# Local layers: first feed-forward matrix in two rounded parts, row norms by logarithm and exponential

## The chip, the cores and the metric

The kernel runs on one core of a Trainium2 chip. The metric is the device time of one execution in microseconds (us). Engines in the rows are named PE (TensorE), PEld (its weight loads), DVE (VectorE), ACT (ScalarE), POOL (GpSimd) and SP (SyncE, which issues DMAs).

## The reference, cut to what matters

Four blocks follow each other, each with a residual and a layer norm: an attention with relative positions, a stack of six local layers, a causal attention, and a mixture of experts. The change lies almost wholly in the six local layers, which for 16 sequences of 256 rows and 128 columns compute:

```python
def attn_layer(x, Wqkv, qs, ksc, Wo):      # 16 heads of 64
    q, k, v = heads(x @ Wqkv)
    q = l2norm(q) * qs                     # t / max(norm(t), 1e-12)
    k = l2norm(k) * ksc
    q = q * cos * scale + rotate_half(q) * sin * scale
    k = k * cos * inv + rotate_half(k) * sin * inv
    return local_attention(q, k, v) @ Wo   # window of 32, scale 8.0

def ffn_layer(x, g, bln, W1, b1, W2, b2):  # W1 is 128 x 682, W2 341 x 128
    xn = (x - mu) / jnp.sqrt(var + 1e-05) * g + bln
    a, gate = jnp.split(xn @ W1 + b1, 2, -1)
    return a * jax.nn.gelu(gate, approximate=False) @ W2 + b2

for i in range(6):
    x = attn_layer(shift_tokens(x), ...) + x
    x = ffn_layer(shift_tokens(x), ...) + x
```

## The kernel before

All activations of the 16 sequences stay on the chip, in `X`. The local layers run sequence by sequence and layer by layer: a *pass* `one_pass(l, b)` belongs to layer `l` and sequence `b` (`n = l * 16 + b`), and 96 of them follow each other. Each pass has four *slots*, j = 0 to 3. A step is one half of the heads for one half of the rows (128 rows, 8 heads of queries and 8 of keys), so a sequence has four steps. In slot j the engines work on different steps at once: the projections of step j + 4, turned queries and keys and scores of step j + 2, probabilities and outputs of step j + 1, and the product with Wo of step j. The feed forward of the sequence before (`f = n - 1`) is spread over the slots. Passes 2 to 13 of each layer are a hardware loop; the others are written out.

There is no scheduler. Each engine has its own program, written out in order, and semaphores join them. The order on each engine in a slot:

- TensorE (`one_pass`): projections of queries and keys (`by_high` L1544 and L1545, `by_low` L1549), turning of the scaled rows (`turn_qk` L1533), projection of values, in slot 2 `first_gates`, in slot 3 `first_values`, then `turn_outputs` (L1579, waits for the query copy two steps on), `turn_probs` (L1593), `scores` (L1612), in slot 2 `last_gate_and_value`, `through_wo` (L1631), `outputs` (L1641), and at the end of slot 1 `turn_xn` (L1652). `through_w1` (L1658) multiplies two chunks of the first matrix, in float32, with the turned normalised rows `xnT`; it is called three times a pass. `ffn_output` (L1681) stands in slot 0 of the pass after.
- ScalarE: `exps` (L1821), `mask` (L1825), `squares` (L1798), the copies of turned queries and keys (L1785, L1787), values (L1807), in slot 2 two `gated` (L1843), turned outputs and probabilities (L1816, L1812); at the end of slot 1 `scale_x` (L1832) and `turned_xn` (L1837), in slot 2 the third `gated`, in slot 3 `turned_x` (L1780). In slot 2 a tiny GELU (L1793) ahead of the squares loads the GELU's table; the first exponential after it loads its own again.
- VectorE: `rotate` (L1943 to L1945, sums of squares L1950), maxima and their subtraction (L1962, L1966, into `b_pr`), `floor_squares` (L1956), `normalise`, `residual`, and the feed forward's statistics and gates.
- GpSimd: for each step `normalise_rows`: the sum of the rotation's two products (L1416), the inverse norms by a power of -0.5 (L1420), in the first step of a pass the feed forward's `deviations` (L1433 to L1438, whose last result `shift` ScalarE needs for `scale_x`), and the scaling of the rows (L1427). After the second step `split_x` (L1444, L1447) makes the rounded high and low part of a later sequence's input. In the last two passes of a layer it also makes the low parts of the next layer's projection weights (`low_part`, L1410, 128 x 512 each) and the tables with gains.
- SyncE: loads, window copies of values, and the shifted copy `x_shifted` (`shift_x`). `load_w1` for a layer is issued in the layer's second pass, once the values of the layer before are through.

For the input and the projection weights the kernel already uses two rounded parts (type `F32R`, "fp32r" in the rows): x·w is computed as high·high + high·low + low·high. TensorE waits at each step's first use of the new layer's weights for `w_low`, which counts the low parts, six a layer.

Of the kernel before, what the change touches and what calls it, by code (L numbers as in the profile page):

```python
# [57 lines left out]
def shape_constants():  # L58
# [39 lines left out]
    c["rot_cos"] = lay(cos * scale * f(8), cos * inv)  # L98
    c["rot_sin"] = lay(sin * scale * f(8), sin * inv)
# [32 lines left out]
def build_program(nc, T, out):  # L132
    ctx = ExitStack()
    with ctx:
# [106 lines left out]
        with ExitStack() as st:  # L241
# [42 lines left out]
            ev_wr, tabs = sem("a_ev_wr"), sem("a_tabs")  # L284
# [6 lines left out]
            ROW, EXT, PRODUCT, PP, CHAIN = 2, 3, 4, 5, 6  # L291
            E_HIGH, E_LOW, EK_MASKED, EK_HIGH, EK_LOW = 6, 7, 8, 9, 11

            x_copied, queries_ok = sem("a_x_copied"), sem("a_queries_ok")
            far = sem("a_far")
# [6 lines left out]
            with nc.Block() as block:  # L302
                @block.sync
                def _(sp):
# [6 lines left out]
                    for name, t in (("L0_attn_Ek", 1), ("L0_attn_Eq", 2)):  # L311
# [12 lines left out]
                    sp.dma_start(tab_ext.rearrange("t d r -> d t r"), ext[:, 0:2, :]).then_inc(tabs, 16)  # L324
                    sp.wait_ge(tabs, 16)
                    sp.dma_start(ek_row, bass.AP(tab_ext, HD * NREX + KREV,
                                                 [[0, P // HD], [NREX, HD], [1, KJ]])).then_inc(tabs, 16)
                    sp.dma_start(eq_tab[:, :], bass.AP(tab_ext, 0, [[1, LB], [NREX, HD], [1, TABW]])).then_inc(tabs, 16)
                    sp.wait_ge(tabs, 16 * 3)
# [3 lines left out]
                def _(act):  # L333
# [6 lines left out]
                    for t in range(LT):  # L340
                        act.dma_start(e_col[:, t:t + 1], bass.AP(T["L0_attn_Eq"].tensor, t * (NREL - 1) * HD,
                                                                 [[0, P // HD], [1, HD], [1, 1]]),
                                      allow_slow_non_contiguous=True).then_inc(far, 16)
                        row = (1 - t) * (NREL - 1)
                        act.dma_start(ev_far[:, t, :], T["L0_attn_Ev"][row:row + 1, :].broadcast_to((P, HD))
                                      ).then_inc(far, 16)
# [8 lines left out]
                def _(pool):  # L355
# [11 lines left out]
                    pool.wait_ge(far, 16 * 2 * LT)  # L367
# [7 lines left out]
                    pool.wait_ge(ld_w, 48)  # L375
# [7 lines left out]
                    pool.wait_ge(tabs, 16 * 3)  # L383
# [773 lines left out]
        with ExitStack() as st:  # L1157
# [9 lines left out]
            w1 = sb(st, "b_w1", [P, 2 * FF])  # L1167
            w2 = sb(st, "b_w2", [P, 3, D])
# [8 lines left out]
            rnorm = sb(st, "b_rnorm", [P, 2, 16])  # L1177
            t1, t2 = sb(st, "b_t1", [P, 2, 16, BD]), sb(st, "b_t2", [P, 2, 16, BD])
# [45 lines left out]
            masked = sem("b_masked")  # L1224

            N_WA, N_LN, N_W1, N_W2 = 3, 2, 5, 3
            SEQ = 4
# [29 lines left out]
            with nc.Block() as block:  # L1257
# [148 lines left out]
                def _(pool):  # L1406
# [6 lines left out]
                    def normalise_rows(n, s, deviations_of=None):  # L1413
# [46 lines left out]
                    def one_pass(l, b, front=True, ffn=True, last_front=False, new_front=False, x_follows=True,  # L1460
                                 last_norm=False):
# [1396 lines left out]
```

## Time and profile before

| | us |
|---|---|
| median of 3 runs | 5004.2 |
| lowest, highest | 5002.4, 5008.55 |
| the profiled execution's own time | 5004.04 |
| its span, from first to last instruction | 5002.2 |
| PE busy | 4560.0 |
| PEld busy | 3754.4 |
| VectorE busy | 3696.6 |
| ScalarE busy | 3399.6 |
| GpSimd busy | 3558.5 |

Busy time is what the engine's instructions cover in the span; matmuls are pipelined and their ends are modelled, so for them the distance between starts tells more than a duration. The time outside the span is 1.8 us. The mean granted TensorE clock was 0.972 of full speed. The local layers take the span from about 960 to 4230 us, ahead of them is the first attention, behind them the causal attention and the experts.

### The profile page before, as it was taken

How to read it: one execution, taken by the hardware profiler on the slowest of the kernel's cores; microseconds unless marked ns; L12 is line 12 of the kernel's file. 1: busy time of each engine (PE TensorE's matmuls, PEld its weight loads, DVE VectorE, ACT ScalarE, POOL GpSimd, SP SyncE). 2: the span in 40 equal slices, each digit the busy share in tenths (PEclk: the TensorE clock that was granted, in tenths of full speed). 3: DMA queues.
4: the chain of work that ended last, by engine and by line, in shares of the span. 5: the costliest groups of instructions: out<-in, count | busy, mean ns of one | idle time of the engine just before them, and what ended most of it. 6: DMA issues, size and time to landing. Idle time of an engine off the chain costs nothing. (4 is left out here: it accounts for less than half of the span.)

```text
span 5002.2 us, 202509 instructions
## 1 busy us (share of the span) xinstructions
PE 4560.0 (91%) x82160; PEld 3754.4 (75%) x82160; DVE 3696.6 (74%) x7406; ACT 3399.6 (68%) x6468; POOL 3558.5 (71%) x2507
## 2 busy tenths in 40 slices
PE   6888888799999999999999999999999997888879
PEld 4777777678887888788877887888877885555557
DVE  4877777788887888778877888788877884555544
ACT  3565565577777777777777777777777774666664
POOL 3334334499999999989999999999999995222212
PEclk8999999999999999999999999999999998999889
DMA  4333333332223222332223222322232221000000
GB/s 119 98 101 112 98 104 105 93 84 69 68 69 88 70 68 69 73 83 69 69 72 85 70 69 70 87 69 70 68 74 70 69 68 40 1 0 0 0 1 18
DMA packets 500471, 338.98 MB, mean 68 GB/s; under 512 B 222559, under 2 KB 489084, under 8 KB 499213
## 3 DMA queue, kind: packets, MB, share of 16 engines
q1 hardware_dynamic: 493566, 320.55, 25.3%
q10 hardware_dynamic: 6544, 13.18, 0.9%
q8 instruction: 280, 4.59, 0.4%
q14 instruction: 81, 0.66, 0.0%
HBM read 60.06 MB, written 54.58 MB: 23 GB/s over the span
## 5 line engine op out<-in xcount | busy, mean ns | idle before, releaser
L1420 POOL TENSOR_TENSOR b_rnorm<-b_ss,neghalf 128x16 f32<-128x16 f32 x384 | 1118.2, 2912 | 25.1 <-DVE b_ss L1956 21.5
L1416 POOL TENSOR_TENSOR b_rot<-b_t 128x1024 f32<-128x1024 f32 x384 | 909.5, 2369 | 75.3 <-DVE b_t L1945 74.6
L1943 DVE TENSOR_TENSOR b_t<-psum,b_cosg 128x1024 f32<-128x1024 f32 x384 | 469.6, 1223 | 426.3 <-ACT b_sq L1798 420.3
L1427 POOL TENSOR_TENSOR b_qk<-b_rot,b_rnorm 128x1024 f32<-128x1024 f32 x384 | 731.0, 1904 | 42.8 <-POOL b_rnorm L1420 2.7
L1544 PE MATMUL psum<-b_w_hi,b_xT_parts 128*128 128x512 f32 x1152 | 528.0, 458 | 28.6 <-issue 19.3
L1798 ACT ACTIVATE b_sq<-psum 128x1024 f32<-128x1024 f32 x384 | 392.1, 1021 | 221.9 <-PE psum L1549 221.5
L1950 DVE TENSOR_REDUCE b_ss_floor<-b_sq 128x16 f32<-128x1024 f32 x384 | 464.3, 1209 | 0.0
L1549 PE MATMUL psum<-b_w_hi,b_xT_parts 128*128 128x512 f32 x1152 | 459.9, 399 | 0.0
L1545 PE MATMUL psum<-b_w_lo,b_xT_parts 128*128 128x512 f32 x1152 | 457.3, 397 | 0.0
L1631 PE MATMUL psum<-shared,b_oT 128*128 128x128 f32 x3072 | 425.2, 281 | 0.8 <-ACT b_oT L1816 0.8
L1533 PE MATMUL psum<-ident,b_qk 128*128 128x128 f32 x3072 | 405.9, 275 | 21.3 <-DVE b_o L1982 15.3
L1533 PEld LDWEIGHTS psum<-ident,b_qk 128*128 128x128 f32 x3072 | 360.0, 142 | 84.9 <-DVE b_o L1982 25.7
L1631 PEld LDWEIGHTS psum<-shared,b_oT 128*128 128x128 f32 x3072 | 380.0, 191 | 27.2 <-issue 1.5
L1821 ACT ACTIVATE b_pr<-b_pr 128x512 f32<-128x512 f32 x384 | 241.6, 629 | 217.0 <-DVE b_pr L1966 197.2
L1982 DVE TENSOR_TENSOR b_o<-psum,b_rs 128x256 f32<-128x256 f32 x768 | 326.2, 425 | 26.5
L1641 PE MATMUL psum<-b_v_win,b_prT 64*32 64x65 f32 x24576 | 336.4, 225 | 3.9 <-issue 3.8
L1612 PE MATMUL psum<-b_kT,b_qTs 64*32 64x64 f32 x24576 | 333.3, 224 | 0.4 <-issue 0.4
L1658 PE MATMUL psum<-b_xnT,b_w 128*128 128x256 f32 (+1 forms) x1152 | 306.2, 388 | 16.8 <-DVE b_hid L2006 2.9
L1612 PEld LDWEIGHTS psum<-b_kT,b_qTs 64*32 64x32 f32 x24576 | 270.6, 105 | 61.5 <-issue 49.4
L1641 PEld LDWEIGHTS psum<-b_v_win,b_prT 64*32 64x32 f32 x24576 | 272.1, 105 | 51.5 <-issue 5.0
L1816 ACT COPY b_oT<-psum 128x512 f32<-128x512 f32 x384 | 232.5, 605 | 112.6 <-PE psum L1579 112.5
L2357 ACT ACTIVATE c_probs<-psum,c_nmax 128x256 f32<-128x256 f32 x512 | 200.9, 482 | 117.5 <-DVE c_nmax L2424 117.2
(271 smaller groups left out, 11545.8 us busy)
## 6 DMA issues: line engine op xcount, KB each, us to landing
b_v_win<-b_v SPq DMA_DIRECT2D x2304, 65.0 KB
keyed<-shared SPq DMA_DIRECT2D x64, 768.0 KB, 4.7
b_v_win<-b_v SPq DMA_DIRECT2D x1152, 32.5 KB
a_logits<-keyed SPq DMA_DIRECT2D x128, 160.0 KB, 3.1
oa<-XR SPq DMA_DIRECT2D x1024, 2.0 KB
xcur<-X SPq DMA_DIRECT2D x111, 128.0 KB, 4.3
shared<-in_L_ffn_Wqkv_dram ACTq DMA_DIRECT2D x6, 1536.0 KB
a_logits<-keyed SPq DMA_DIRECT2D x64, 128.0 KB, 3.0
```

The costliest lines, as they stand in the source:

```text
L1416: nc.gpsimd.tensor_tensor(rot[:, i, :, :], t1[:, i, :, :], t2[:, i, :, :], ALU.add).then_inc(rot_done, 1)
L1420: nc.gpsimd.tensor_tensor(rnorm[:, i, :], ss[:, i, :], neghalf[:, :], ALU.pow).then_inc(rn_done, 1)
L1427: nc.gpsimd.tensor_tensor(qk[:, i, :, :], rot[:, i, :, :], rnorm[:, i, :, None].broadcast_to((P, 16, BD)), ALU.mult).then_inc(qk_done, 1)
L1533: last = nc.tensor.transpose(r[:, p * P:(p + 1) * P], qk[:, s % 2, a * 8 + 2 * p:a * 8 + 2 * p + 2, :].rearrange("p h d -> p (h d)"), iden ...
L1544: nc.tensor.matmul(r, xT_hi[:, ts], w_hi[:, piece(hg, i)], start=True, stop=False)
L1545: nc.tensor.matmul(r, xT_hi[:, ts], w_lo[:, piece(hg, i)], start=False, stop=False)
L1549: return nc.tensor.matmul(r, xT_lo[:, ts], w_hi[:, piece(hg, i)], start=False, stop=True)
L1612: last = nc.tensor.matmul(bank[3 + j][qs, p * 2 * WIN:(p + 1) * 2 * WIN], qTs[at, p, qs], kT[at, p, keys], start=False, stop=(p == 3), ski ...
L1631: last = nc.tensor.matmul(bank_c[:, 0:D], oT[:, p, :], wo[:, 4 * (s % SEQ // 2) + p, :], start=(p == 0), stop=(p == 3))
L1641: last = nc.tensor.matmul(r[qs, p * (BD + 1):(p + 1) * (BD + 1)], prT[at, p, qs], v_win[at, s % NV, c, p, :], start=(p == 0), stop=(p == 3 ...
L1943: nc.vector.tensor_tensor(t14, x4, tab(cosg, slice(0, BD), BD), ALU.mult)
L1950: nc.vector.tensor_reduce(ss_floor[:, t, :, 0], sq[:, :].rearrange("p (h d) -> p h d", d=BD), AX.X, ALU.add).then_inc(ss_done, 1)
```

## The change

The feed forward's first product is computed like the projections. Once a layer GpSimd splits `w1` into `w1_hi` and `w1_lo` (`split_w1`), behind `split_x` in the second step of the layer's second pass. ScalarE reads the turned normalised rows twice, once into `xnT` in float32 and once rounded into `xn_parts[:, 0]`, and GpSimd makes the low part (`split_xn`) in the second step of every pass, between the rotation's sum and the norms. `through_w1` issues three rounded matmuls for each chunk instead of one in float32, and `first_gates` waits for the low part and, in a layer's first feed forward, for the split of `w1`. The counter `w_low` now counts eight a layer.

The inverse norms of the rows are computed as exp(-0.5 · ln(s)) on ScalarE (`guess_norms`), followed by one step of Newton's method on GpSimd, r·(3 - s·r²), which gives twice the inverse norm; the tables of the rotation take the factor 0.5. The set of activation tables that holds both functions is loaded by name at the start and in slot 3 of each pass with a feed forward. In the first attention, two semaphores are dropped and their loads counted on others (L284 to L383).

```diff
-    c["rot_cos"] = lay(cos * scale * f(8), cos * inv)
-    c["rot_sin"] = lay(sin * scale * f(8), sin * inv)
+    c["rot_cos"] = lay(cos * scale * f(4), cos * inv * f(0.5))
+    c["rot_sin"] = lay(sin * scale * f(4), sin * inv * f(0.5))
...
-                    pool.wait_ge(far, 16 * 2 * LT)
+                    pool.wait_ge(ld_w, 16 * (3 + 2 * LT))
...
-                    def normalise_rows(n, s, deviations_of=None):
+                    def normalise_rows(n, s, deviations_of=None, split_of=None):
                         m, i = n * SEQ + s + 1, s % 2
                         pool.wait_ge(t_done, m)
                         nc.gpsimd.tensor_tensor(rot[:, i, :, :], t1[:, i, :, :], t2[:, i, :, :],
                                                 ALU.add).then_inc(rot_done, 1)
-
-                        pool.wait_ge(floor_done, m)
-                        nc.gpsimd.tensor_tensor(rnorm[:, i, :], ss[:, i, :], neghalf[:, :],
-                                                ALU.pow).then_inc(rn_done, 1)
+                        if split_of is not None:
+                            split_xn(split_of)
+                        pool.wait_ge(guess_done, 2 * m)
+                        nc.gpsimd.tensor_tensor(rn_step[:, i, :], ss[:, i, :], rn_guess[:, i, :], ALU.mult).then_inc(step_done, 1)
+                        pool.wait_ge(step_done, 3 * m - 2)
+                        nc.gpsimd.tensor_tensor(rn_step[:, i, :], rn_step[:, i, :], rn_guess[:, i, :], ALU.mult).then_inc(step_done, 1)
+                        pool.wait_ge(step_done, 3 * m - 1)
+                        nc.gpsimd.tensor_tensor(rn_step[:, i, :], three[:, :], rn_step[:, i, :], ALU.subtract).then_inc(step_done, 1)
+                        pool.wait_ge(step_done, 3 * m)
+                        nc.gpsimd.tensor_tensor(rnorm[:, i, :], rn_step[:, i, :], rn_guess[:, i, :], ALU.mult).then_inc(rn_done, 1)
...
+                    def split_xn(f):
+                        pool.wait_ge(xnT_done, 2 * f + 2)
+                        nc.gpsimd.tensor_tensor(xn_parts[:, 1, :], xnT[:, :], xn_parts[:, 0, :].bitcast(F32),
+                                                ALU.subtract).then_inc(xn_split, 1)
+
+                    def split_w1(l):
+
+                        both = slice(0, 2 * FF)
+                        pool.wait_ge(w1_ld, (l + 1) * (16 * N_W1))
+                        nc.gpsimd.tensor_tensor(w1_hi[:, both], w1[:, :], ones[:, 0:1].broadcast_to((P, 2 * FF)),
+                                                ALU.mult).then_inc(w_low, 1)
+                        pool.wait_ge(w_low, l * N_LOW + 7)
+                        nc.gpsimd.tensor_tensor(w1_lo[:, both], w1[:, :], w1_hi[:, both].bitcast(F32),
+                                                ALU.subtract).then_inc(w_low, 1)
...
                             if front:
-                                normalise_rows(n + 1, s, n - 1 if ffn and s == 0 else None)
+                                normalise_rows(n + 1, s, n - 1 if ffn and s == 0 else None,
+                                               n - 1 if ffn and s == 1 else None)
                             if last_front and s == 0:
                                 layer_gains(l + 1)
                             if x_follows and s == 1:
                                 split_x(n + 2)
+                            if new_ffn and s == 1:
+                                split_w1(l)
...
                             w, k = FCH[c % 3], (c // 3) * FF + P * (c % 3)
-                            last = nc.tensor.matmul(ffn_bank[0:w, j * S:(j + 1) * S], w1[:, k:k + w], xnT[:, :],
-                                                    start=(j == 0), stop=(j == 1), skip_group_check=True)
+                            w += w % 2
+                            for i, (weight, part) in enumerate(((w1_hi, 0), (w1_lo, 0), (w1_hi, 1))):
+                                last = nc.tensor.matmul(ffn_bank[0:w, j * S:(j + 1) * S], weight[:, k:k + w],
+                                                        xn_parts[:, part, :], start=(j == 0 and i == 0),
+                                                        stop=(j == 1 and i == 2), skip_group_check=True)
                         last.then_inc(h_full, 1)
 
                     def first_gates(f, new_ffn):
                         if new_ffn is not None:
-                            pe.wait_ge(w1_ld, (new_ffn + 1) * (16 * N_W1))
-                        pe.wait_ge(xnT_done, f + 1)
+                            pe.wait_ge(w_low, (new_ffn + 1) * N_LOW)
+                        pe.wait_ge(xn_split, f + 1)
                         through_w1(3, 4)
...
+                    def guess_norms(s, m):
+
+                        i = s % 2
+                        act.wait_ge(floor_done, m)
+                        nc.scalar.activation(log_ss[:, i, :], ss[:, i, :], ACT.Ln).then_inc(guess_done, 1)
+                        act.wait_ge(guess_done, 2 * m - 1)
+                        nc.scalar.activation(rn_guess[:, i, :], log_ss[:, i, :], ACT.Exp, scale=-0.5).then_inc(guess_done, 1)
+
...
                         nc.scalar.activation(xnT[:, :], ffn_bank[:, 0:S], ACT.Identity, bias=lnb[:, 0:1],
                                              scale=lng[:, 0:1]).then_inc(xnT_done, 1)
+                        nc.scalar.activation(xn_parts[:, 0, :], ffn_bank[:, 0:S], ACT.Identity, bias=lnb[:, 0:1],
+                                             scale=lng[:, 0:1]).then_inc(xnT_done, 1)
...
+                            if j == 3 and ffn:
+                                nc.scalar.preload_act_table_set(LOG_EXP)
                             if ok(j + 1):
                                 exps(j + 1, m + 1)
+                            if ok(j + 3):
+                                guess_norms(j + 3, m + 3)
```

## Rows read from the trace of the kernel before

**Rows 1.** Busy time in a stretch: us, each engine busy (x count), clock, DMA share, GB/s

```profile
2000.00:2500.00 500.00, 482.79 (x10019) 403.29 (x10017) 400.76 (x860) 371.19 (x645) 467.70 (x278) 0.99 0.30 73
```

**Rows 2.** TensorE's waits, 1000 to 4230: in total, times, longest us

```profile
PE psum L1579 <- ACT b_qTs L1785: 20.1, 86, 0.3
...
PE psum L1533 <- POOL b_qk L1427: 3.8, 4, 1.7
```

**Rows 3.** Timeline of TensorE, one pass: start us, us, line, out<-in, count, idle before

```profile
2418.81 0.44 PE L1652 MATMUL psum<-ident,b_xn 128*128 128x128 f32 x2
...
2422.05 1.03 PE L1658 MATMUL psum<-b_xnT,b_w 128*128 128x256 f32 x4
2423.33 0.66 PE L1579 MATMUL psum<-ident,b_o 128*128 128x128 f32 x4 [0.25 <-ACT b_qTs L1785]
...
2425.57 1.09 PE L1658 MATMUL psum<-b_xnT,b_w 128*85 128x256 f32 x4
...
2431.34 1.02 PE L1658 MATMUL psum<-b_xnT,b_w 128*128 128x256 f32 x4
2432.20 0.60 PE L1579 MATMUL psum<-ident,b_o 128*128 128x128 f32 x4
```

**Rows 4.** Timeline of ScalarE, the same pass

```profile
2419.29 0.57 ACT L1837 ACTIVATE b_xnT<-psum,b_lnb,b_lng 128x256 f32<-128x256 f32 x1 [1.56 <-PE psum L1652]
2419.75 0.62 ACT L1821 ACTIVATE b_pr<-b_pr 128x512 f32<-128x512 f32 x1
...
2422.70 0.58 ACT L1785 COPY b_qTs<-psum 128x512 f32<-128x512 f32 x1
...
2424.64 0.87 ACT L1843 ACTIVATE b_gel<-psum,b_b 128x256 f32<-128x256 f32 x2
...
2429.97 1.02 ACT L1798 ACTIVATE b_sq<-psum 128x1024 f32<-128x1024 f32 x1 [0.37 <-PE psum L1549]
```

**Rows 5.** Timeline of TensorE in phase one

```profile
604.56 0.27 PE L654 MATMUL psum<-a_k_diag,a_e_parts 128*128 128x256 f32 x1
...
604.91 0.40 PE L650 MATMUL psum<-a_k_diag,a_q_parts 128*128 128x256 f32 x2
```

**Rows 6.** One line, L650: duration ns least, median, most

```profile
L650 PEld LDWEIGHTS psum<-a_k_diag,a_q_parts x512: 186/189/337, 67.3 to 947.2; 128*128 128x128 f32 x171
```

**Rows 7.** Groups of instructions, 1000 to 4230: count, busy us, mean ns

```profile
L1793 ACT ACT_TABLE_LOAD x94 | 120.6, 1283 | 1.7
...
L1410 POOL TENSOR_TENSOR b_w_lo<-shared,b_w_hi 128x512 fp32r<-128x512 f32 x30 | 38.2, 1287 | 0.0
...
L1793 ACT ACTIVATE b_no_gate<-ones 128x1 f32<-128x1 f32 x94 | 19.2, 204 | 1.1
```

**Rows 8.** The page's costliest groups: count, busy us, mean ns, idle before

```profile
L1420 POOL TENSOR_TENSOR b_rnorm<-b_ss,neghalf 128x16 f32<-128x16 f32 x384 | 1118.2, 2912 | 25.1 <-DVE b_ss L1956 21.5
...
L1427 POOL TENSOR_TENSOR b_qk<-b_rot,b_rnorm 128x1024 f32<-128x1024 f32 x384 | 731.0, 1904 | 42.8 <-POOL b_rnorm L1420 2.7
```

**Rows 9.** Timeline of GpSimd, the same pass as rows 3

```profile
2414.90 0.69 POOL L1436 TENSOR_TENSOR b_frstd<-b_fvar,neghalf 128x2 f32<-128x2 f32 x1
2415.68 0.20 POOL L1438 TENSOR_TENSOR b_shift<-b_less_mean,b_frstd 128x2 f32<-128x2 f32 x1
```

**Rows 10.** Timeline of TensorE, last pass of the first layer

```profile
1514.53 0.41 PE L1652 MATMUL psum<-ident,b_xn 128*128 128x128 f32 x2 [4.24 <-ACT b_xn L1832]
```

**Rows 11.** Timeline of ScalarE, last pass of the first layer

```profile
1513.51 0.88 ACT L1832 ACTIVATE b_xn<-b_x_shifted,b_shift,b_frstd 128x128 f32<-128x128 f32 x2 [5.13 <-POOL b_shift L1438]
```

**Rows 12.** Busy time behind that gap; the last but two numbers are clock, DMA share

```profile
1514.00:1518.00 4.00, 3.47 (x13) 2.87 (x14) 0.00 (x0) 3.38 (x6) 4.00 (x3) 0.63 0.38 89
```

**Rows 13.** Timeline of GpSimd, second pass of the second layer

```profile
1581.11 2.39 POOL L1416 TENSOR_TENSOR b_rot<-b_t 128x1024 f32<-128x1024 f32 x1
...
1588.37 0.61 POOL L1444 TENSOR_TENSOR b_x_parts<-xcur,ones 128x256 fp32r<-128x256 f32 x1
```

**Rows 14.** Timeline of TensorE, second pass of the second layer

```profile
1585.14 1.03 PE L1658 MATMUL psum<-b_xnT,b_w 128*128 128x256 f32 x4
```

More of the change, by code:

```diff
@@ L291, in build_program @@
             ROW, EXT, PRODUCT, PP, CHAIN = 2, 3, 4, 5, 6
+            TURNED, TABLES = 4, 6
             E_HIGH, E_LOW, EK_MASKED, EK_HIGH, EK_LOW = 6, 7, 8, 9, 11
             x_copied, queries_ok = sem("a_x_copied"), sem("a_queries_ok")
-            far = sem("a_far")
             def window_blocks(mt, hh):
@@ L342, in _ @@
                                                                  [[0, P // HD], [1, HD], [1, 1]]),
-                                      allow_slow_non_contiguous=True).then_inc(far, 16)
+                                      allow_slow_non_contiguous=True).then_inc(ld_w, 16)
                         row = (1 - t) * (NREL - 1)
                         act.dma_start(ev_far[:, t, :], T["L0_attn_Ev"][row:row + 1, :].broadcast_to((P, HD))
-                                      ).then_inc(far, 16)
+                                      ).then_inc(ld_w, 16)
                     act.dma_start(X[:, :, :], x_in).then_inc(ld_x, 16)
@@ L1167, in build_program @@
             w1 = sb(st, "b_w1", [P, 2 * FF])
+            w1_hi, w1_lo = sb(st, "b_w1_hi", [P, 2 * FF + 2], F32R), sb(st, "b_w1_lo", [P, 2 * FF + 2], F32R)
+            xn_parts = sb(st, "b_xn_parts", [P, 2, S], F32R)
             w2 = sb(st, "b_w2", [P, 3, D])
@@ L1177, in build_program @@
             rnorm = sb(st, "b_rnorm", [P, 2, 16])
+            log_ss, rn_guess, rn_step = (sb(st, f"b_{n}", [P, 2, 16]) for n in ("log_ss", "rn_guess", "rn_step"))
+            three = sb(st, "b_three", [P, 16])
             t1, t2 = sb(st, "b_t1", [P, 2, 16, BD]), sb(st, "b_t2", [P, 2, 16, BD])
@@ L1223, in build_program @@
             gel_done, hid_done = sem("b_gel_done"), sem("b_hid_done")
-            masked = sem("b_masked")
+            masked, xn_split = sem("b_masked"), sem("b_xn_split")
+            guess_done, step_done = sem("b_guess_done"), sem("b_step_done")
+            LOG_EXP = "natural_log_exp_and_others"
             N_WA, N_LN, N_W1, N_W2 = 3, 2, 5, 3
+            N_LOW = 6 + 2
             SEQ = 4
@@ L1469, in one_pass @@
                                 split_x(n + 2)
+                            if new_ffn and s == 1:
+                                split_w1(l)
                             if ffn and s == 0 and not front:
                                 deviations(n - 1)
+                            if ffn and s == 1 and not front:
+                                split_xn(n - 1)
                             if last_front and s == 1:
@@ L1486, in _ @@
                     nc.gpsimd.memset(zero[:, :], 0.0)
+                    for parts in (w1_hi, w1_lo):
+                        nc.gpsimd.tensor_tensor(parts[:, 2 * FF:], ones[:, 0:2], ones[:, 0:2], ALU.subtract)
+                    nc.gpsimd.memset(three[:, :], 3.0)
                     nc.gpsimd.memset(ss_floor[:, :, :, 1], 1e-24).then_inc(filled, 1)
```

27 lines of the change are left out of this document (14 added, 13 removed).

## The prediction, as it was put on record

> **What bounds the kernel now.** I began with the busy times of a stretch inside the local layers, where nearly all of the change lies: of 500 us TensorE works 482.8 and GpSimd 467.7 [rows 1]. The reader is to see that both look like a bound. The table of waits decides: in the whole stage TensorE waited for GpSimd's scaled rows 4 times, 3.8 us in all, but for ScalarE's copy of the queries, at L1579, 86 times in 96 passes [rows 2]. GpSimd works 94% of the time, yet ahead of need.
>
> A pass (one sequence, four slots) takes about 33 us. Its chain, from the timelines: TensorE turns the normalised rows at 2418.81 (L1652). Projections, turned rows and the first gates follow, the gates from 2422.05; L1579 starts at 2423.33, just as the queries' copy ends, 2422.70 + 0.58 [rows 3, 4]. From 2419.29 on ScalarE has no gap: turned rows, exponentials, a table load, squares, queries. So in slot 2 the chain runs through ScalarE; a second place is the pair of gates at 2425.57, right behind the GELU's end, 2424.64 + 0.87 [rows 3, 4]. From there to the next L1652 it is TensorE's own work.
>
> **The change, part by part.** *TensorE.* A pair of chunks is 4 instructions now; the pair at 2431.34 lets L1579 begin at 2432.20: 0.86 us [rows 3]. After it is 6 rounded matmuls of 256 columns. Phase one has such matmuls, same size of weights and columns: three steps from 604.56 to 604.91, 0.117 us each [rows 5]. 6 x 0.117 = 0.70, a gain of 0.16 a pair (bounds: 0, if rounding gained only what more loads take, and 0.2). Of three pairs the one ahead of L1579 gains nothing, as ScalarE ends later; two count: -0.32 us a pass.
>
> Here a rule speaks against the change. The Trainium skill, "TensorE: Matmul & The Clock Gate", Part 3, says that a weight load overlaps running matmuls only where its row group differs; all loads here use all rows, and by it each of the six would pay load and matmul. The trace has loads of 189 ns there [rows 6] and yet matmuls 0.117 us apart, so it disagrees; as a mechanism it is rival 4.
>
> *ScalarE, slot 2.* Added ahead of the queries' copy: (a) the second reading of the turned rows; from such an instruction to the next is 2419.75 - 2419.29 = 0.46 us [rows 4]; (b) logarithm and exponential of 128x16. The nearest row is the 128x1 activation, 204 ns [rows 7]; the second waits for the first: 0.20 + 0.06 (my estimate) + 0.20, less 0.06 that neighbours overlap: 0.40 us. Together 0.86 (bounds: 0.1, if VectorE's b_pr comes later than the second reading, and 1.2). The chain through L1579 and the GELU moves by as much. In the other slots (b) falls into the idle time ahead of squares, smallest in slot 3 with 0.37 us [rows 4]; without that cover it would cost up to 0.4 more. Table loads stay two a pass, 1.28 us each [rows 7]: the named set is loaded where the exponential's was. Behind (b) in ScalarE's queue stand mask, squares and query copy, for which TensorE waits in slot 2 alone.
>
> Sum of an ordinary pass: +0.86 - 0.32 = +0.54 us.
>
> *GpSimd, each step.* The power (2.91 us, 384 times [rows 8]) gives way to four operations in a row. One of 128x2 takes 0.20, and 2415.68 - (2414.90 + 0.69) = 0.09 lies ahead of a dependent one [rows 9]: 4 x 0.29 = 1.2 us. So each step is 1.7 us shorter. The low part of the input, half of a 512-column subtraction of 1.29 [rows 7] and some overhead, 0.75, is added once a pass. It waits for ScalarE's second reading: 2419.29 + 0.46 + 0.57 = 2420.3, split by 2421.1, needed at 2422.05; cover 0.9. Behind it stand the norms of that step, wanted a slot later. In an ordinary pass nothing waited for GpSimd, so its gain is worth nothing.
>
> *Where GpSimd did bind.* In the last pass of each of the first five layers it also makes low parts of the next layer's weights. There ScalarE waited 5.13 us for the shift [rows 11] and TensorE 4.24 us for ScalarE [rows 10]; five such gaps. 5 steps x 1.7 us of relief ahead of it end the gap. Behind it the granted clock was 0.63 over 4 us [rows 12], so partly 1.2 GHz, about 0.6 us of lost work more: 5 x 4.8 = -24 us. What is late next there is TensorE itself. (Passes whose x_shifted is late by a DMA stay long.)
>
> *A new wait.* Once a layer w1 itself is split: 682 columns, high part 0.61 x 682/256 = 1.6 [rows 13], low part 1.29 x 682/512 = 1.7 us [rows 7]. It stands last in GpSimd's second step of the pass, behind rotation, the input's low part, norms, scaling and x, while TensorE's first gates wait for it with the rest of slot 2 behind them in its queue, and nothing queued there frees GpSimd. In such a pass of before: rotation ends 1583.5 [rows 13]; then low part 1584.2, norms 1585.4, scaling (1.90 [rows 8]) 1587.3, x (0.61 + 0.7) 1588.7, w1 1592.0; the gates started at 1585.14 [rows 14]. TensorE stands 6.8 us. The clock then falls as after the 4 us gaps; longer, I take 2 us. Off goes ScalarE's usual share of slot 2 (0.4 ahead of L1579, 0.5 in the smaller gaps), since ScalarE has time: +7.9, with the lighter pairs +7.6. Six layers: +46 us (bounds 30 and 56).
>
> *Rest.* At the end the second reading 0.46 and the split 0.75 stand on the chain, against three lighter pairs at the low clock: 0. At the start one table load of 1.28 against shorter norms: -1. In phase one the same loads are awaited on other semaphores, once: 0. Tables with other factors: none.
>
> Sum: 77 ordinary passes x 0.54 = 42; 12 with late x_shifted x 0.1 = 1; -24; +46; -1: +64 us. Against the profiled execution's own 5004.04 us that is 5068; the median of the runs, 5004.2, differs by nothing that counts.
>
> **The rivals.**
> 1. *ScalarE's additions hide* (the other side: not slower). If in slot 2 VectorE's b_pr comes 0.8 us or more behind the turned rows, the second reading and part of the norms run inside a wait, and an ordinary pass changes by 0.1 - 0.32. 77 x -0.22 = -17; -17 + 1 - 24 + 46 - 1 = +5: 5009. The point is a growth of 0.2 us. For it: VectorE is 80% busy and feeds ScalarE each slot [rows 1]. Against: at 2419.75 ScalarE's row has no idle time ahead of it [rows 4]. Chance 0.12.
> 2. *The split of w1 is cheap*, GpSimd being so far ahead that it ends near the gates: +46 becomes about +5, 5027. Against: its step needs ScalarE's reading of the same slot. Chance 0.08.
> 3. *ScalarE's chain is longer* (small dependent activations at twice my price): 1.2 instead of 0.86, 77 x 0.34 = +26, and in slot 3 uncovered, 89 x 0.14 = +12: 5106. Chance 0.10.
> 4. *Weight loads not hidden*: 6 x (0.189 + 0.117) = 1.84 a pair, 1.14 more than forecast; the first pair hides behind ScalarE, two count: 89 x 2.3 = +205, 5273. Chance 0.02.
> 5. *The change doesn't do what it says*: logarithm and exponential take different tables, and each step loads two more, 2.57 us. ScalarE's 371.2/60 = 6.2 us a step [rows 1] become 9.2 against 8.2 of the pass's quarter, which is the bound then: 384 x 1.1 = +420, 5430. The Trainium skill, "ScalarE: Activation LUTs", on table sets, names one set that holds both; no row of before shows it. Chance 0.03.
>
> **How the numbers follow.** Forecast 0.65. From 5010 to 5112 lie the forecast with its bounds, rivals 2 and 3 and the upper half of rival 1; outside are the other half, 4 and 5. A measurement tells 0.2% (10 us) from no change. Faster needs rival 1 and a short split of w1 together, 0.05; same 0.10; slower 0.85.
>
> **What would show it.** A pass 0.5 us longer; L1579 waiting some 1.3 us for the queries' copy behind the first gates; as many table loads as before at two places; rounded pairs of 0.70 us; the four norm operations within 1.2 us; no gap ahead of the turned rows in a layer's last pass; once a layer a gap of 6 to 7 us ahead of the first gates with a lower clock behind it. Wrong it would be if those gates never wait, or if squares start later than the projections allow in slots 0, 1 and 3.

## The result, and the profile after

| us | before | after |
|---|---|---|
| median of the runs | 5006.38 (5002.40 to 5019.39) | 5081.01 (5072.94 to 5082.54, 4 runs) |
| ratio of the times, 95% interval | | 1.0134 (1.0122 to 1.0147) |
| span of the profiled execution | 5002.2 | 5079.1 |
| GpSimd busy | 3558.5 | 2892.7 |
| ScalarE busy | 3399.6 | 3572.3 |

The changed kernel is slower by 75 us in the medians, by 77 in the profiled spans, and by 67 (61 to 74) by the ratio, which weighs all runs and not the middle one. The stretch inside the local layers, to be held against [rows 1]:

```profile
2000.00:2500.00 500.00, 469.31 (x9895) 398.28 (x9899) 395.50 (x851) 394.00 (x773) 361.15 (x469) 0.99 0.29 73
```

GpSimd lost 107 of its 468 us, and ScalarE, 23 us heavier, is what the pass now feels. TensorE is busy 13 us less in the same 500 us; some 8 of them are only passes that no longer fit, since at 33.4 us a pass 15.0 fit where at 32.8 it was 15.2. A pass itself gives TensorE some 0.3 us less to do. The waits of TensorE from 1000 to 4300 us, to be held against [rows 2], say for whom it stands (line, releaser and its line, total, times, longest):

```profile
PE psum L1621 <- ACT b_qTs L1830: 95.0, 91, 1.2
PE psum L1702 <- POOL b_w_lo L1469: 38.6, 6, 6.5
PE psum L1694 <- ACT b_xn L1885: 18.9, 11, 8.1
...
PE psum L1702 <- POOL b_xn_parts L1459: 5.3, 8, 1.9
```

The first line is the old wait for the queries' copy, 20.1 us before and 95.0 now. The second is new: six times, once a layer, the first gates stand for the low part of w1. The input's low part, the last line, comes late 8 times in 96.

**An ordinary pass.** TensorE, ScalarE and GpSimd in the pass that begins at 2418 us, as [rows 3], [rows 4] and [rows 9] show it of before:

```profile
2418.28 0.44 PE L1694 MATMUL psum<-ident,b_xn 128*128 128x128 f32 x2
...
2421.52 0.28 PE L1702 MATMUL psum<-b_xn_parts,b_w_hi 128*128 128x256 f32 x1
...
2423.61 0.65 PE L1621 MATMUL psum<-ident,b_o 128*128 128x128 f32 x4 [1.22 <-ACT b_qTs L1830]
...
2431.46 0.28 PE L1702 MATMUL psum<-b_xn_parts,b_w_hi 128*128 128x256 f32 x1
...
2432.17 0.60 PE L1621 MATMUL psum<-ident,b_o 128*128 128x128 f32 x4
```

```profile
2418.76 0.57 ACT L1890 ACTIVATE b_xnT<-psum,b_lnb,b_lng 128x256 f32<-128x256 f32 x1 [1.70 <-PE psum L1694]
2419.22 0.56 ACT L1892 ACTIVATE b_xn_parts<-psum,b_lnb,b_lng 128x256 fp32r<-128x256 f32 x1
2419.67 0.63 ACT L1866 ACTIVATE b_pr<-b_pr 128x512 f32<-128x512 f32 x1
2420.19 0.21 ACT L1872 ACTIVATE b_log_ss<-b_ss 128x16 f32<-128x16 f32 x1
2420.43 0.21 ACT L1874 ACTIVATE b_rn_guess<-b_log_ss 128x16 f32<-128x16 f32 x1
2420.67 1.28 ACT L1838 ACT_TABLE_LOAD   x1
...
2422.97 0.58 ACT L1830 COPY b_qTs<-psum 128x512 f32<-128x512 f32 x1
```

```profile
2419.86 0.74 POOL L1459 TENSOR_TENSOR b_xn_parts<-b_xnT,b_xn_parts 128x256 fp32r<-128x256 f32 x1 [0.46 <-ACT b_xn_parts L1892]
2420.72 0.22 POOL L1432 TENSOR_TENSOR b_rn_step<-b_ss,b_rn_guess 128x16 f32<-128x16 f32 x1
...
2421.63 0.23 POOL L1438 TENSOR_TENSOR b_rnorm<-b_rn_step,b_rn_guess 128x16 f32<-128x16 f32 x1
```

From L1694 to L1621 it is 5.33 us; before it was 2423.33 - 2418.81 = 4.52 [rows 3]. Of ScalarE's row, 0.45 is the second reading (2419.67 - 2419.22). From the start of the scores' exponential to the table load it is now 1.00 us (2419.67 to 2420.67); in the kernel before it was 0.64, from 2419.75 [rows 4] to the load in this row of before:

```profile
2420.39 1.28 ACT L1793 ACT_TABLE_LOAD   x1
```

So the two small functions add 0.36. A rounded pair lets the next line start after 0.71 (2431.46 to 2432.17) where it was 0.86. GpSimd's split is over at 2420.60, 0.9 us ahead of the gates, and its four norm operations, of which the first and the last are shown, take 1.14 us together.

**Once a layer.** GpSimd in the second pass of the second layer, and TensorE there; before, in [rows 13] and [rows 14]:

```profile
1597.55 2.37 POOL L1427 TENSOR_TENSOR b_rot<-b_t 128x1024 f32<-128x1024 f32 x1
...
1605.08 1.32 POOL L1466 TENSOR_TENSOR b_w_hi<-b_w,ones 128x682 fp32r<-128x682 f32 x1
1606.48 1.62 POOL L1469 TENSOR_TENSOR b_w_lo<-b_w,b_w_hi 128x682 fp32r<-128x682 f32 x1
```

```profile
1608.16 0.58 PE L1702 MATMUL psum<-b_xn_parts,b_w_hi 128*128 128x256 f32 x1 [6.44 <-POOL b_w_lo L1469]
```

The low part ends at 1608.10 and the gates begin 0.06 us behind it. Busy time from there on (columns as in [rows 12]) shows what the gap costs in clock:

```profile
1608.00:1612.00 4.00, 3.84 (x55) 3.51 (x60) 0.00 (x0) 1.83 (x4) 2.42 (x2) 0.50 0.33 83
1612.00:1616.00 4.00, 4.00 (x125) 3.50 (x114) 2.22 (x7) 2.58 (x5) 0.00 (x0) 0.94 0.23 54
```

For 4 us the granted clock is 0.50, the lower level of 1.2 GHz, after TensorE had stood for 6.4 us; a clock of 0.94 over the next 4 us means another 0.5 us at that level. TensorE starts at 1608.16, so 4.3 us of its work run at half speed, which costs about 2.1 us.

**In the last pass of a layer** the gap of [rows 10] is gone; there TensorE goes from the outputs straight to the normalised rows:

```profile
1527.13 0.86 PE L1683 MATMUL psum<-b_v_win,b_prT 64*32 64x65 f32 x64
...
1527.92 0.44 PE L1694 MATMUL psum<-ident,b_xn 128*128 128x128 f32 x2
```

**Where the 77 us lie.** Each pass has one turning of the normalised rows, 96 of them in both traces. Here a pass is the distance from one turning to the next, which makes 95; in mid-layer it is 32.8 us before and 33.4 after (medians). Compared pass by pass, after less before:

| part of the span | us |
|---|---|
| ahead of the first turning (1048.1 before, 1049.7 after) | +1.6 |
| 6 passes with the layer's first gates (+8.1, 6.1, 5.0, 4.6, 7.6, 5.5) | +36.8 |
| the 6 passes behind them | -3.8 |
| distances that end with the gap in the last pass of the first five layers (-3.5, -3.3, -3.3, -4.4, -3.2) | -17.8 |
| the other 78 passes, 0.60 each | +47.1 |
| behind the last turning (786.6 before, 799.5 after) | +12.9 |

### The profile page after: what moved, and what is told of

The parts are those of the page before. It is cut to its first block and busy times, and to the rows that moved or that the text cites. A ratio compares the mean times of both kernels' runs of the same rounds, so it can differ in the third digit from the quotient of the medians.

```text
span 5079.1 us, 207085 instructions
## 1 busy us (share of the span) xinstructions
PE 4543.1 (89%) x82736; PEld 3786.4 (75%) x82736; DVE 3694.7 (73%) x7406; ACT 3572.3 (70%) x7335; POOL 2892.7 (57%) x3770
## 5 line engine op out<-in xcount | busy, mean ns | idle before, releaser
L1575 PEld LDWEIGHTS psum<-ident,b_qk 128*128 128x128 f32 x3072 | 355.9, 140 | 83.4 <-DVE b_o L2042 32.8
L1621 PE MATMUL psum<-ident,b_o 128*128 128x128 f32 x1536 | 244.3, 282 | 97.7 <-ACT b_qTs L1830 95.0
L1702 PE MATMUL psum<-b_xn_parts,b_w_hi 128*128 128x256 f32 (+1 forms) x1152 | 267.7, 294 | 59.9 <-POOL b_w_lo L1469 38.6
L1654 PEld LDWEIGHTS psum<-b_kT,b_qTs 64*32 64x32 f32 x24576 | 270.1, 106 | 62.4 <-issue 50.4
L1432 POOL TENSOR_TENSOR b_rn_step<-b_ss,b_rn_guess 128x16 f32<-128x16 f32 x384 | 86.1, 224 | 389.7 <-ACT b_rn_guess L1874 381.5
```

The source lines that it names most:

```text
L1575: last = nc.tensor.transpose(r[:, p * P:(p + 1) * P], qk[:, s % 2, a * 8 + 2 * p:a * 8 + 2 * p + 2, :].rearrange("p h d -> p (h d)"), iden ...
L1654: last = nc.tensor.matmul(bank[3 + j][qs, p * 2 * WIN:(p + 1) * 2 * WIN], qTs[at, p, qs], kT[at, p, keys], start=False, stop=(p == 3), ski ...
```

## The experiments

Each kernel starts from the changed one, and none of the eight leaves out a part of the computation. The kernel before, run beside the first four that follow in time (norms_only, w1_only, norms_late, high_on_pool), took 5012.9 us, beside the other four 5012.0. So that kernels of different runs can be compared, a difference from before is its ratio's: 1% is 50 us, and by this measure the change itself is worth +67. Beside it stands the growth of the local layers alone, from the first to the last turning of rows in the profiled execution: +62.4 for the change.

**One part alone, norms.** The first matrix stays a float32 product, with no second reading, no split of the input and no split of w1; the norms go by logarithm.

```diff
-                            if new_ffn and s == 1:
-                                split_w1(l)
...
-                            for i, (weight, part) in enumerate(((w1_hi, 0), (w1_lo, 0), (w1_hi, 1))):
...
+                            last = nc.tensor.matmul(ffn_bank[0:w, j * S:(j + 1) * S], w1[:, k:k + w], xnT[:, :],
...
```

> The feed forward's product stays in float32, as before; only the norms by logarithm and exponential are taken. Theory (ScalarE's chain in slot 2 sets an ordinary pass, GpSimd bound only in each layer's last pass): 0.36 to 0.40 us more in some 77 passes, +30, and five gaps of 4 us with their slow clock gone, -24: 5 to 10 us over the kernel before. Rival (GpSimd's relief is worth something in every pass): clearly faster than before, by 20 us or more. Rival (nearly all of the loss is the norms'): +40 or more.

Measured: 5035.27 us, ratio 1.0045 (1.0030 to 1.0059), 22 more; local layers +15.2. An ordinary pass is 0.39 longer (the median of the 60 in mid-layer, and so below), close to the 0.36 read above. The five distances that end with the gap give back 17.4, and the five behind them, where the slow clock lay, another 2.7; set against 0.39 more in each of these ten, the gaps are worth 24.0, as counted. The mechanism is as forecast, the size is not: 5 to 10 us were expected. The longer pass was counted 77 times, 30 us, but nearly all 95 distances carry it, which makes 37. The rest up to the ratio's 22 (15 to 29) lies outside the local layers; behind them the profiled execution took 795.8 us for before's 786.6, in code that does not differ (last section).

**The other part alone, w1.** The rounded product with its splits, the norms by power as before.

```diff
-                        pool.wait_ge(guess_done, 2 * m)
-                        nc.gpsimd.tensor_tensor(rn_step[:, i, :], ss[:, i, :], rn_guess[:, i, :], ALU.mult)...
...
+                        pool.wait_ge(floor_done, m)
+                        nc.gpsimd.tensor_tensor(rnorm[:, i, :], ss[:, i, :], neghalf[:, :],
+                                                ALU.pow).then_inc(rn_done, 1)
...
-                                guess_norms(j + 3, m + 3)
...
```

> The first matrix in two rounded parts as in the changed kernel, the norms by a power as before. Theory: 0.46 - 0.30 us in 77 passes, +12; the wait for the split of w1 lengthened by the longer norms, 6 x 9.3 = +56; the gaps in each layer's last pass stay and grow by GpSimd's 0.75 us a pass and what it waits: +15. Sum +83 over the kernel before, more than the changed kernel's +75. Rival (the two parts add up without touching each other): 75 less what the norms alone cost, about +65.

Measured: 5082.04 us, ratio 1.0140 (1.0123 to 1.0157), 70 more; local layers +69.4. That is less than the 83 expected: the six passes with the first gates grew by 48.2 where 56 was counted, and the five distances that end in a last pass by 4.8 where it was 15. TensorE's waits, 1000 to 4300:

```profile
PE psum L1616 <- ACT b_qTs L1825: 61.1, 81, 0.9
PE psum L1697 <- POOL b_w_lo L1464: 50.6, 6, 9.7
PE psum L1689 <- ACT b_xn L1880: 40.0, 18, 6.8
```

The stall for w1 is up to 9.7 us long here (6.5 in the changed kernel), and the last pass of a layer keeps its gap:

```profile
1525.83 0.66 PE L1689 MATMUL psum<-ident,b_xn 128*128 128x128 f32 x2 [4.26 <-ACT b_xn L1880]
```

So the gap of [rows 10] goes by the shorter norms, not by the rounded product. The two parts add up in an ordinary pass (0.39 + 0.22 = 0.61, and the change's own is 0.60), but not where GpSimd binds. The local layers grow by 15.2 and 69.4, 84.6 in sum, and by 62.4 with both: 22 less. Of these 14 lie in the six passes with the first gates (2.6 and 48.2 alone, 36.8 together) and 5 in the last passes (-17.4 and +4.8 alone, -17.8 together). The shorter norms shorten the stall that the other part brings: 9.7 us at most without them, 6.5 with them.

**Norms behind the copies.** If ScalarE's chain is what the ordinary pass pays for, the logarithm and exponential of slot 2 can stand behind the query and key copies.

```diff
-                            if ok(j + 3):
+                            if ok(j + 3) and not (j == 2 and ffn):
                                 guess_norms(j + 3, m + 3)
...
                             if ok(j + 2) and gates_follow:
                                 mask(j + 2)
+                            if ok(j + 3) and gates_follow:
+                                guess_norms(j + 3, m + 3)
```

> The changed kernel with logarithm and exponential of slot 2 issued behind the copies of queries and keys and the mask, instead of ahead of the squares. Theory: 0.36 us leaves the chain of each pass with a feed forward: 90 x 0.36 = 32 us faster than the changed kernel, +43 over the kernel before; GpSimd's norms of that step come 2.5 us later and nobody waits for them. Rival (a pass is longer by TensorE's own work, 36 matmuls where 24 were): no difference to the changed kernel. Rival (GpSimd's later norms bind): slower than it.

Measured: 5626.17 us, ratio 1.1219 (1.1201 to 1.1238), 611 more, the largest miss of the study. ScalarE's timeline says why:

```profile
2698.07 0.61 ACT L1878 COPY psum<-b_masks 128x512 f32<-128x512 f32 x1
2698.70 1.28 ACT L1872 ACT_TABLE_LOAD   x1
2699.99 0.21 ACT L1872 ACTIVATE b_log_ss<-b_ss 128x16 f32<-128x16 f32 x1
2700.23 1.28 ACT L1874 ACT_TABLE_LOAD   x1
2701.52 0.22 ACT L1874 ACTIVATE b_rn_guess<-b_log_ss 128x16 f32<-128x16 f32 x1
2702.23 1.28 ACT L1898 ACT_TABLE_LOAD   x1
```

By then the GELU's table is in place. The logarithm loads one set, the exponential another, and the GELU loads its own again: three more loads, 3.84 us a pass, all ahead of the first GELU, for which TensorE now waits 402.6 us in 89 waits (1000 to 4850 us). The stall for w1 grows too, from 38.6 to 75.9 us, and the mean granted clock falls from 0.967 to 0.925; how the rest of the 611 divides was not tried. This run did not test the chain; it tested rival 5, in the one place where the named set was not loaded. The Trainium skill, "ScalarE: Activation LUTs", "Table sets: the hidden batching unit", counts one load for a logarithm and then an exponential, since one set holds both; here each took a set of its own, two loads, and only in the changed kernel, where that set is asked for by name, does the trace agree with the rule.

**The high part on GpSimd.** The same question without tables: ScalarE's second reading goes, GpSimd rounds xnT itself.

```diff
+                        nc.gpsimd.tensor_tensor(xn_parts[:, 0, :], xnT[:, :], ones[:, 0:1].broadcast_to((P, S)),
+                                                ALU.mult).then_inc(xn_split, 1)
...
-                        nc.scalar.activation(xn_parts[:, 0, :], ffn_bank[:, 0:S], ACT.Identity, bias=lnb[:, 0:1],
...
```

> The changed kernel with the rounded high part of the input made by GpSimd from the float32 copy (two operations of 0.6 and 0.74 us) instead of by ScalarE's second reading. Theory: 0.46 us leaves ScalarE's chain in slot 2, and the parts are ready 0.7 us ahead of the first gates: 80 x 0.46 = 37 us faster than the changed kernel, +38 over the kernel before. Rival (TensorE's own work is the bound): no difference. Rival (first gates now wait for GpSimd): the gain is lost in a wait ahead of the first gates.

Measured: 5040.08 us, ratio 1.0061 (1.0037 to 1.0085), 31 more; local layers +33.4. Against the changed kernel it is 37 less by the ratios, as expected, and 29 less in the local layers. TensorE's waits, 1000 to 4300:

```profile
PE psum L1624 <- ACT b_qTs L1833: 60.3, 82, 1.0
PE psum L1705 <- POOL b_w_lo L1472: 42.9, 6, 7.4
```

The wait for the queries falls from 95.0 to 60.3, an ordinary pass from +0.60 to +0.15, while the stall for w1 grows by 4.3, as GpSimd now has one operation more ahead of it. One 0.45 us reading on ScalarE is worth 0.45 us a pass: the queries' copy is what the pass waits for, and nothing hides the reading.

**The split of w1 early.** w1 is loaded in the last pass of the layer before, two passes earlier, and split at the start of the layer's second pass. Shown is the move of the split; the load's move and the waits that go with it are left out.

```diff
                         for s in range(SEQ):
+                            if new_ffn and s == 0:
+                                split_w1(l)
...
-                            if new_ffn and s == 1:
-                                split_w1(l)
```

> The changed kernel, but w1 is loaded in the last pass of the layer before, and GpSimd splits it at the start of the layer's second pass, one slot ahead, instead of behind the second step's rows. Theory: the gap of 6.4 us ahead of the first gates and the slow clock behind it go, six times: 6 x 6 = 36 to 45 us faster than the changed kernel, +35 over the kernel before. Rival (the pass is late by another wait that ends just as late, GpSimd's low part of the input or its shift): half of it or less. The 3.3 us of the split may make GpSimd's shift later in that pass: then a gap ahead of the turned rows takes its place.

Measured: 5045.96 us, ratio 1.0062 (1.0045 to 1.0079), 31 more; local layers +28.3. Against the changed kernel that is 36 less by the ratios and 34 in the local layers. GpSimd and TensorE in the second layer's second pass:

```profile
1572.09 1.32 POOL L1474 TENSOR_TENSOR b_w_hi<-b_w,ones 128x682 fp32r<-128x682 f32 x1
```

```profile
1590.06 0.28 PE L1710 MATMUL psum<-b_xn_parts,b_w_hi 128*128 128x256 f32 x1
```

No wait for b_w_lo is left. The six passes go from +36.8 to -1.6, the pass behind them from -3.8 to -2.0, and an ordinary pass stays at +0.59. So the stall, gap, clock and all, is worth 34 to 38 us (36.8 + 1.6 in its own passes), and nothing else hung on it.

**Norms ahead.** The logarithm and exponential of slot 2 move into slot 1, ahead of the turned rows, where ScalarE has idle time and its table is the right one; VectorE's sums are put ahead of its maxima there, so that they are ready.

```diff
-                            if ok(j + 3):
+                            if ok(j + 3) and not (j == 2 and ffn):
                                 guess_norms(j + 3, m + 3)
...
                                 scale_x(f)
+                                if ok(j + 4):
+                                    guess_norms(j + 4, m + 4)
                                 turned_xn(f)
...
+                            early = j == 1 and ffn
+                            if ok(j + 4) and early:
+                                floor_squares(j + 4, m + 4)
...
```

> The changed kernel with the logarithm and exponential that stood in slot 2 issued in slot 1, ahead of the reading of the turned rows, where ScalarE waits 1.7 us for TensorE and the right table set is still loaded; VectorE's small operation for it moves ahead of its maxima there. Theory: 0.36 us leaves the chain of each pass with a feed forward: some 30 us faster than the changed kernel, +45 over the kernel before. Rival (a pass is longer by TensorE's own work): no difference. Rival (VectorE's maxima, 0.15 us later, are on the chain): 15 us faster only.

Measured: 5047.48 us, ratio 1.0062 (1.0045 to 1.0079), 31 more; local layers +37.7. Against the changed kernel that is 36 less by the ratios and 25 in the local layers. An ordinary pass goes from +0.60 to +0.26 and the wait for the queries to 61.4 us:

```profile
PE psum L1621 <- ACT b_qTs L1830: 61.4, 85, 1.0
```

This is what norms_late was meant to show: 0.36 us on ScalarE's chain is 0.34 us of the pass.

**All three moves together,** the high part on GpSimd, the early split and the norms ahead.

> The changed kernel with all three moves: high part of the input by GpSimd, norms of slot 2 in slot 1, w1 split one slot earlier. If the three costs are separate: 0.3 us less than before in some 80 passes (lighter gates), -25; gaps of each layer's last pass gone, -18; no gap once a layer; about 4965, 40 us faster than the kernel before. If one of them only hid another: between 4990 and 5010.

Measured: 4990.94 us, ratio 0.9955 (0.9938 to 0.9972), 22 less than before and 90 less than the changed kernel: it beats both. The local layers are 24.1 shorter than before. The ordinary pass is 0.16 us shorter than before's, the six passes with the first gates come to -1.3, the last passes to -20.3. TensorE's waits from 1000 to 4240 us, and one ScalarE stretch:

```profile
PE psum L1632 <- ACT b_qTs L1841: 36.7, 89, 1.0
PE psum L1705 <- ACT b_xn L1896: 25.8, 16, 6.8
PE psum L1586 <- DVE b_o L2053: 25.5, 32, 1.4
```

```profile
2408.26 0.22 ACT L1883 ACTIVATE b_log_ss<-b_ss 128x16 f32<-128x16 f32 x1 [0.73 <-DVE b_ss L2027]
...
2409.07 0.57 ACT L1901 ACTIVATE b_xnT<-psum,b_lnb,b_lng 128x256 f32<-128x256 f32 x1 [0.35 <-PE psum L1705]
```

The logarithm stands in idle time now (0.73 us ahead of it, 0.35 behind the pair). The three moves brought about half of the 40 us expected. What is missing are the lighter gates: they were to bring 25 us in some 80 passes, but the 78 passes that the table above has in one row come to -0.6 in all, -8 in the 60 of mid-layer (0.16 each where 0.3 was expected) and +7.5 in the 18 near a layer's ends. Why those 18 grew was not tried.

**Norms ahead, and nothing else.** Is the rounded product worth having once nothing waits for its helpers?

> The feed forward's product in float32 as before; norms by logarithm and exponential, those of slot 2 in slot 1. Theory: nothing is added to the chain of an ordinary pass, and GpSimd's relief ends the gaps of each layer's last pass: 15 to 20 us faster than the kernel before, 35 faster than the run with the norms alone. The distance to the run with all three moves is then what the two rounded parts are worth: about 25 us. Rival (the logarithm and exponential in slots 0, 1 and 3 cost as well): no faster than the kernel before.

Measured: 5001.41 us over 10 runs, ratio 0.9982 (0.9972 to 0.9991), 9 less than before; local layers -10.8. Against norms_only, where the two functions stand in the chain, it is 32 less, as expected (35). An ordinary pass is level with before's (+0.06), the last passes give 19.4. By the distance to all_three the rounded product is worth 13 us, 0.2 a pass (the two intervals touch at 0.9972, and the local layers of the profiled executions differ by 13 too), not the 25 expected: two pairs are 0.30 lighter, but the outputs' matmuls take some 0.09 back (last section).

## Why the prediction was right

The time, 5081, lies in the range from 5010 to 5112, 13 above the forecast of 5068, and the forecast's case is the one that happened: ScalarE's chain in slot 2 lengthened each pass, the gaps in the last passes went, and the split of w1 brought a new one. That the sum inside the local layers came out so close, 62.4 for 65, is in part luck: the stall was put 9 us too high and the passes without any gap 6 us too low. Its steps in order:

- **The bound.** The chain of slot 2 through ScalarE's copy of the queries is what an ordinary pass pays for. Shown three times: 0.45 us taken off gave 0.45 (high_on_pool), 0.36 gave 0.34 (norms_ahead), and adding the two functions gave 0.39 (norms_only). The wait for the queries' copy was to be 1.3 us and was 1.22. Rival 1 (additions hidden, 5009) is refuted by the same runs.
- **An ordinary pass,** +0.54 forecast. ScalarE +0.45 and +0.36 (0.46 and 0.40), two pairs -0.30 (-0.32); that makes +0.51. Measured +0.60; the 0.09 that remain have the size of what the outputs' matmuls lost (last section), which the sum did not have. That this is where they went was not shown. Rival 3 (small dependent functions at twice the price) is refuted by the 0.36, and the same functions in slots 0, 1 and 3 cost next to nothing, as norms_ahead_only's +0.06 shows.
- **Late x_shifted** (+0.1 in 12 passes) was wrong: in the 78 passes that were left, these among them, the mean is 0.60 like the ordinary ones. Some 6 us.
- **The gaps in the last passes,** -24 forecast, and right. The gap did end, and by the shorter norms (w1_only keeps it). From turning to turning the distances shrink by 17.8 only, because they carry an ordinary pass's +0.60 like all others (the forecast's 77 and 12 passes hold them too), and because they end with the gap: the slow clock fell into the distance behind. Those five sum to -0.2 where five ordinary ones would make +3.0. So the gaps were worth 17.8 + 0.2 + 10 x 0.60 = 24.0 us, 4.2 of wait and 0.6 of clock each.
- **The stall for w1,** +46 forecast, +36.8 measured in its passes. Its own parts were right: the gap 6.44 us for 6.8, from the rotation's end to the end of the low part 8.2 us for 8.5, the clock about 2.1 us for 2. Mis-sized was what they were added to. The forecast set 7.6 us on top of a pass of before as if it were an ordinary one of 32.8; but before's six passes already took 33.6, 35.2, 36.8, 37.0, 34.9 and 36.6, which is 17 us more in all, and the stall took the place of part of that. Five of the six ended in a wait of TensorE for ScalarE's normalised rows (0.4, 0.7, 3.5, 1.2 and 2.6 us), and in the changed kernel none does. The third layer, before and after:

```profile
2154.25 0.69 PE L1652 MATMUL psum<-ident,b_xn 128*128 128x128 f32 x2 [3.50 <-ACT b_xn L1832]
```

```profile
2183.52 0.44 PE L1694 MATMUL psum<-ident,b_xn 128*128 128x128 f32 x2
```

In the changed kernel the six take 41.3 to 42.5 us, on average 8.4 above an ordinary pass of its own, which is the gap and its clock. With the stall taken out (split_early) they are still 12 us above six ordinary ones, and in three of them the wait for the normalised rows is back (0.3, 1.8 and 0.5 us). Which of before's other short waits went with the stall was not followed up. By the same experiment the stall is worth 34 to 38 us. Rival 2 (5027) is refuted: GpSimd was not ahead.
- **Both parts in one place.** The prediction gave GpSimd's relief no worth in an ordinary pass and the splits no worth in the last pass; with both parts in place that stands (-17.8 for -17.4 of the norms alone). But in the passes with the first gates the shorter norms shorten the stall too, 14 us over the six, which its own chain of times held implicitly (norms over at 1585.4) and no term named.
- **Start, end, phase one,** -1 forecast. Ahead of the local layers +1.6; behind them +12.9, in code that the change leaves as it was but for the last feed forward, which takes 20.9 us in both. This term is where the 13 us between 5068 and 5081 lie. It depends on the execution of before that it is held against: that one took 5004.0 us, while 21 further runs of the same kernel had medians of 5012.9 and 5012.0 (last section). By the ratio of the runs the change is worth 67 us, 3 above the forecast's 64.
- **Rival 4,** loads not hidden: refuted. A pair takes 0.71 us, not 1.84, though its loads have a mean of 194 ns and use all rows. The Trainium skill, "TensorE: Matmul & The Clock Gate", Part 3, has in its list of what overlaps that a load overlaps matmuls only in another row group; here, as in [rows 5, 6], the trace disagrees. Just ahead of that list the same Part also names the background weight buffer as a target for which a load is pulled ahead, which the prediction did not weigh; no row tells which buffer these loads went to.
- **Rival 5,** a table for each function: the mechanism is real, as norms_late shows at 611 us, and the named load is what avoids it. (Its price in the prediction should read 5424, 5004 + 420.) In the changed kernel the loads are 95 and 94, two a pass (line, count, busy, mean ns, idle before):

```profile
L1910 ACT ACT_TABLE_LOAD x95 | 121.9, 1283 | 1.7
...
L1838 ACT ACT_TABLE_LOAD x94 | 120.6, 1283 | 1.6
```

## What to carry to other kernels

Work taken from an engine that is busy 94% of the time but ahead of need buys nothing except where somebody waits for it, while 0.8 us put on the engine with idle time, just ahead of the copy that the pass waits for, costs 0.8 us in each pass; the same two functions one slot earlier, in idle time, cost next to nothing (0.06). A preparation needed once a layer belongs where its consumer is far off, not behind the last things of the slot in which it is needed. And before a transcendental function is moved on ScalarE, see which table stands there: one misplaced pair cost eight times what the change did. And before a new wait is added to a sum, look at how long the passes are in which it will fall: it may cover waits that they have already.

## What the runs showed of the hardware

**The clock in code that did not change.** The causal attention and the experts are the same instructions in all the kernels, yet with the last feed forward ahead of them, 20.9 to 21.2 us in all the kernels, they took 786.6 us in before's profiled execution and 790.2 to 803.7 in the nine others. Busy time from the last turning of rows to the end (columns as in [rows 12]), of before and of after:

```profile
4215.59:5002.20 786.61, 644.39 (x4954) 452.89 (x4954) 386.97 (x876) 461.44 (x1109) 179.19 (x163) 0.88 0.01 3
```

```profile
4279.60:5079.10 799.50, 657.08 (x4960) 464.78 (x4960) 386.82 (x876) 463.28 (x1111) 180.18 (x164) 0.86 0.01 3
```

VectorE, ScalarE and GpSimd have the same busy time within 2 us; TensorE's grows by 12.7, as long as the stretch itself, at a lower granted clock. A clock between the two levels says how the time is shared: summed over stretches of 5 us, 182 us at the lower level before and 219 after. Over the ten profiled executions this number and the length go together:

| kernel | us at the lower level | us behind the last turning |
|---|---|---|
| before | 182 | 786.6 |
| high_on_pool | 193 | 790.2 |
| norms_ahead | 198 | 792.0 |
| norms_ahead_only | 199 | 792.7 |
| norms_only, w1_only | 209, 209 | 795.8, 796.0 |
| norms_late | 212 | 795.7 |
| all_three | 215 | 798.8 |
| after | 219 | 799.5 |
| split_early | 223 | 803.7 |

That before has the shortest does not make it the change's doing, as the kernel before varies by as much: 13 of its runs took from 5001.6 us at a mean clock of 0.972 to 5017.5 at 0.966. Why the clock is low more often in one execution than in another was not tried. Such a stage moved the whole time by up to 17 us between two profiles, so a difference of 10 is not to be read without it.

**The outputs' matmuls spread.** The same 24576 matmuls of 64x65, by line over the whole span (count, busy, mean ns), before and after:

```profile
L1641 PE MATMUL psum<-b_v_win,b_prT 64*32 64x65 f32 x24576 | 336.4, 225 | 3.9 <-issue 3.8
```

```profile
L1683 PE MATMUL psum<-b_v_win,b_prT 64*32 64x65 f32 x24576 | 344.8, 225 | 2.5 <-issue 2.4
```

A single one has the same mean, but together they cover 8.4 us more, 0.09 us a pass. It goes with the rounded product: 336.4 before, 338.2 and 338.3 in the two kernels with a float32 product, 343.1 to 345.1 in those with rounded parts (norms_late aside: 360.1, at its lower clock). The cause stays open.

**Tables.** A load took 1.28 us every time, and the function behind it began 0.01 to 0.02 us after its end, as in norms_late's rows. The Trainium skill, "ScalarE: Activation LUTs", "What ACT_TABLE_LOAD costs", gives the same 1283 ns for the load and adds a drain of 1380 ns for each switch; no row here shows the drain, neither behind the load nor ahead of it (0.02 to 0.03 us there).
